# A constant product ahead of each score unit of the second layer, in a two-layer gated attention kernel

## The chip, the cores and the metric

One core of one Trainium2 chip. The metric is the device time in microseconds (us). The engines are named as in the profile: PE is TensorE (PEld its weight loads), DVE is VectorE, ACT is ScalarE, POOL is GpSimd, SP is SyncE.

## The reference

Sixteen sequences of 128 rows and 128 features go through two gated blocks. Each block is a cross-attention to a context of 120 rows (16 heads of 8), added to x with a gate, and then a feed-forward part, added with a gate. The feed-forward of layer 0 is a mixture of 8 experts of which two are taken, that of layer 1 a mix of each row with the one before it. Only layer 0 masks the keys.

```python
x = x + tanh(g_xattn[0]) * L0_xattn(layernorm(x), ctx, ctx, mask, ...)   # q, k, v, softmax over 120 keys, out
x = x + tanh(g_ffn[0])   * L0_moe(layernorm(x), ...)
x = x + tanh(g_xattn[1]) * L1_xattn(layernorm(x), ctx, ...)              # no mask
x = x + tanh(g_ffn[1])   * L1_mix(layernorm(x), ...)                     # sigmoid(r) * (relu(k)**2 @ Wv)
```

## The kernel before, in words

The whole program is written out by hand, one function per engine, with semaphores between them. Each engine runs its instructions in the order in which they are written. A layer's attention is a pipeline over steps, `s` from 0 to B + 5 (B is 16); sequence `s` of the layer enters the pipeline in step `s`. A step has four units, `r` from 0 to 3, of four heads each.

What TensorE does for one sequence is spread over several steps:
- `scores_q` (L974) computes the scores with the queries as rows, four products of 128x120 into bank 0 or 1. It waits with `max_done` until VectorE's row maximum of two units earlier (L454) has read that bank. Layer 0 adds a product for the mask ahead of the four (L986).
- VectorE splits the negated maxima into three bf16 parts (L471 to L493), TensorE transposes them (`turn_max`, L1022), ScalarE copies them (L771), and GpSimd issues three DMAs that put them as three more rows into the tile of the queries (L368).
- `scores_k` (L994) runs 10 units (LAG) behind `scores_q` and computes the scores again with the keys as rows, with the maxima subtracted by those three rows, into bank 2 or 3. It waits for the DMAs (`m_ld`) and for the exponentials of two units earlier (L780). Layer 0 has a product for the mask here too (L1005).
- `values` (L1038), four steps behind, multiplies by the values; `turn_back` (L1046) turns the result; VectorE divides by the sums (L483, L489); `turn_ctx` (L1055) and `out_proj` (L1059) follow, and VectorE adds to x (L500).

A group is four sequences. While a group is in the pipeline, the next one is prepared, by `prep` (L1061), in 16 units numbered u = 4p + r, spread over four steps. `prep_at` (L196) gives the group and the p of a step: in layer 1 step 0 has p = 1, so that steps 3 and 7 begin a new preparation, and steps 11 to 15 have none. Key products stand in units 1, 4 and 5 (bank 6), the turn of the normalised x in unit 3 (L947, bank 7), query products in units 5, 6 and 8 (L955, L959, bank 7), value projections in unit 10 (L966, bank 6). Bank 7, the query bank, is read by ScalarE after unit 3 (L744) and twice after the query products (L751), and a last time by VectorE in unit 9 (`last_q`, L519). `q_reader` holds the last reader's semaphore and count, and `bank_read` (L926) waits for it.

TensorE runs a unit in this order: `scores_q`, then `turn_max`, then `scores_k`, and then the rest.

Of the kernel before, what the change touches and what calls it, by code (L numbers as in the profile page):

```python
# [40 lines left out]
BF16 = mybir.dt.bfloat16  # L41
# [5 lines left out]
B, S, SK, D = 16, 128, 120, 128  # L47
# [8 lines left out]
UNITS, UH = 4, 4  # L56
# [10 lines left out]
def gated_blocks(nc, x, ctxT, mask, wts, w2sh, bcols, brows, gates, ident, identh, negidh, sel, rank, onesrows, out):  # L67
    ctx = ExitStack()
    with ctx:
        def sb(name, shape, dt=F32):  # L70
            return ctx.enter_context(nc.sbuf_tensor(name, shape, dt))

        def sem(name):
            return ctx.enter_context(nc.semaphore(name))
# [18 lines left out]
        epsT = sb("epsT", [128, GB])  # L93
        warm = sb("warm", [128, GB])
        powT = sb("powT", [128, GB])

        st6 = sb("st6", [S, GB, 6])
        mv = sb("mv", [S, GB, 2])
# [69 lines left out]
        q_st = sem("q_st"); q_ld = [[sem(f"q_ld{i}{f}") for f in range(2)] for i in range(2)]  # L168
        k_done = sem("k_done"); k_evac = sem("k_evac")
        k_st = sem("k_st"); k_ld = [[sem(f"k_ld{i}{f}") for f in range(2)] for i in range(2)]  # L170
        v_done = sem("v_done"); v_evac = sem("v_evac"); bo_done = sem("bo_done"); bo_ok = sem("bo_ok")
        qm_done = sem("qm_done"); max_done = sem("max_done"); nm_ok = sem("nm_ok")
        nt_done = sem("nt_done"); nt_evac = sem("nt_evac"); m_ld = [sem("m_ld0"), sem("m_ld1")]
        km_done = sem("km_done"); exp_done = sem("exp_done")
# [228 lines left out]
        def _(v):  # L403
# [112 lines left out]
            def last_q(G):  # L516
                v.wait_ge(q_done, PARTS * (G + 1))
                L = G // NG
                nc.vector.tensor_scalar(qp[:, PARTS - 1, :], QB[:, :], BC[:, 2 * L:2 * L + 1], None, ALU.add).then_inc(q_evac, 1)  # L519

            ln(0, 0)
            ln_apply(0, 0)
            v.wait_ge(w_in, 64)
# [395 lines left out]
        def _(pe):  # L919
# [6 lines left out]
            def bank_read(reader):  # L926
                if reader[0]:
                    pe.wait_ge(*reader[0])

            def k_proj(G, p):  # L930

                L, g = G // NG, G % NG
                if p == 0:
                    bank_read(kv_reader)
                    mm(KVB[:, 0:GK], W(WK[L]), CT[:, g * GK:(g + 1) * GK], start=True, stop=True).then_inc(k_done, 1)  # L935
                    kv_reader[0] = (k_evac, PARTS * (G + 1))
                else:
                    pe.wait_ge(k_evac, PARTS * G + p)
                    mm(KVB[:, 0:GK], NEG[:, :], kp[:, p - 1, :], start=False, stop=True, skip_group_check=True).then_inc(k_done, 1)
# [231 lines left out]
            for L in range(LAYERS):  # L1171
                for u in range(UNITS):
                    prep(L * NG + 1, u)
                for s in range(B + 6):
                    G, p = prep_at(L, s)
                    for r in range(UNITS):
                        if s < B:
                            scores_q(L * B + s, r)
                        if r == (2 if s > 1 else 0) and 1 <= s < B + 1:
                            turn_max(L * B + s - 1)  # L1180
                        U = UNITS * s + r - LAG
                        if 0 <= U < B * UNITS:
                            scores_k(L * B + U // UNITS, U % UNITS)
                        if r == 1 and 6 <= s < B + 3:
                            out_proj(L * B + s - 6)
                        if r == 0 and 4 <= s < B + 4:
                            values(L * B + s - 4)
                        if r == 2 and 4 <= s < B + 4:
                            turn_back(L * B + s - 4)
                        if r == 3 and 5 <= s < B + 4 or r == 0 and s == B + 4:  # L1190
                            turn_ctx(L * B + s - 5 if r == 3 else L * B + B - 1)
                        if r == 1 and s == B + 4:
                            out_proj(L * B + B - 1)
                        if G is not None:
                            prep(G, UNITS * p + r)
                        if r == 3 and ffn_turn_at(s) is not None:
                            turn(2 * L + 1, ffn_turn_at(s))
                        if L == 0 and r == 0 and ffn_turn_at(s - 1) is not None:
                            logits(ffn_turn_at(s - 1))
                        if L == 1 and s == 0:  # L1200

                            moe_out(NG - 1, r)
                    if L == 0 and s == 1:
                        pe.wait_ge(w_in3, 16)
                        bias_product(0)
                        bias_product(1)
                    if L == 0 and s == 8:
                        pe.wait_ge(w_in2, 80)
                    if L == 0 and s == B + 1:
                        pe.wait_ge(max_done, B * UNITS)  # L1210
                        hidden(0, 0)
                        hidden(0, 1)
                    if L == 1 and s == FILL - 1:
                        kr_mix(0)
                    if L == 1 and s == FILL:
                        kr_mix(1)
                    if s in (B + 2, B + 3):
                        out_proj(L * B + s - 5)
                    if L == 1 and s == FILL:
                        v_mix(0)  # L1220
                if L == 0:
                    pe.wait_ge(exp_done, B * UNITS)
                    turn_gates(0)
                    for k in range(2, NBLK + 1):
                        hidden(0, k)
                    for g in range(NG - 1):
                        for k in range(NBLK + 1):
                            if k < NBLK and (g, k) != (2, 0):
                                gate_rows(g, k)
                            hidden(g + 1, k)  # L1230
                            if (g, k) == (2, 0):
                                gate_rows(g, k)
                            if g == 0 and k == 2:
                                turn(1, NG - 1)
                            if g == 2 and k == 1:
                                turn(2, 0)
                            if g == 2 and k >= 2:
                                q_proj(NG, k - 2)
                        if g == 0:
                            logits(NG - 1)  # L1240
                        if g in (0, 2):
                            turn_gates(g + 1)
                        if g < NG - 1:
                            for i in range(GB):
                                moe_out(g, i)
                        if g == 1:
                            turn_gates(g + 1)
                    for k in range(NBLK):
                        gate_rows(NG - 1, k)

                    pe.wait_ge(h_act, NG * (NBLK + 1))
                    kv_reader[0] = (gt_evac, NG)
                else:
                    v_mix(1)
                    kr_mix(2)
                    turn(3, NG - 1)
                    v_mix(2)
                    kr_mix(NG - 1)
                    v_mix(NG - 1)
# [65 lines left out]
```

## Time and profile before

| | us |
|---|---|
| median of 3 runs | 351.34 |
| lowest and highest run | 346.81 and 354.74 |
| the profiled execution | 347.46 |
| its span, first to last instruction | 345.5 |
| TensorE busy | 277.3 (80%) |
| VectorE busy | 211.6 (61%) |
| ScalarE busy | 171.2 (50%) |
| GpSimd busy | 90.4 (26%) |
| mean granted TensorE clock | 0.922 of full |

The span falls into layer 0's attention (to about 155 us), layer 0's experts (to about 212), layer 1's attention (to about 322) and layer 1's mix. A busy TensorE is not one at its peak, since matmuls overlap in the array and their ends are modelled; so what it waits for, the clock that it was granted, and the chain that ends last say more than its share. The granted clock has two levels: 1.00 is 2.4 GHz, 0.50 is 1.2 GHz.

### The profile page before, as it was taken

What the parts mean: (1) busy time and instruction counts of PE and PEld (TensorE: products, weight loads), DVE (VectorE), ACT (ScalarE), POOL (GpSimd) and SP (SyncE); (2) the same over time, 40 slices, a digit from 0 to 9 for tenths busy, and PEclk for the clock granted to TensorE, in tenths of its full rate; (3) what the DMA queues carried; (4) which work ended last, traced back from release to release, by engine and by line L of the source; (5) the groups of instructions that cost most, each with busy time, mean ns of one, the idle gap of its engine ahead of it and who ended that gap; (6) DMA issues with size and microseconds to landing.
All of it is one profiled execution on the core that took longest, in us unless ns stands there. A gap on an engine that the chain in (4) does not pass through costs nothing.

```text
span 345.5 us, 7867 instructions
## 1 busy us (share of the span) xinstructions
PE 277.3 (80%) x2967; PEld 207.1 (60%) x2980; DVE 211.6 (61%) x653; ACT 171.2 (50%) x330; POOL 90.4 (26%) x156
## 2 busy tenths in 40 slices
PE   1624789999999999868999979898888778888681
PEld 0312556777777777655657557567667567766561
DVE  2412776677584685662557457856877866738752
ACT  1410236656665565636742722446676565576220
POOL 3500233322431241111001102414234333342420
PEclk9955989999999999998999999759999998899878
DMA  8475546443343340000000142433545340000022
GB/s 232 111 196 163 136 135 191 136 129 108 107 132 100 98 117 18 4 2 0 2 0 1 45 124 88 137 126 94 144 130 141 118 127 5 2 5 2 0 63 62
DMA packets 27663, 30.48 MB, mean 88 GB/s; under 512 B 13699, under 2 KB 24804, under 8 KB 26468
## 3 DMA queue, kind: packets, MB, share of 16 engines
q1 hardware_dynamic: 20366, 27.11, 27.2%
q10 hardware_dynamic: 4188, 2.47, 2.8%
q0 software_dynamic: 3072, 0.40, 0.8%
q8 instruction: 24, 0.39, 0.5%
q14 instruction: 13, 0.11, 0.1%
HBM read 22.43 MB, written 7.14 MB: 86 GB/s over the span
## 4 chain that ended last, share of the span: by engine, by line
PE 53%; DVE 16%; DMA 13%; issue 8%; ACT 4%; POOL 3%; ACTq 1%; SPq 1%; another core or an unknown queue 0%; DVEq 0%; POOLq 0%
DMA QS<-nmT 8%; PE bank L1038 6%; PE bank L990 5%; PE bank L1009 5%; PE bank L1125 4%; PE bank L986 3%; PE bank L1005 3%; PE bank L1046 3%; PE bank L1077 3%; DMA QS<-qparts 3%; PE bank L955 2%; PE bank L947 2%; DVE st L427 2%; DVE nmx L454 2%; PE bank L1059 2%
## 5 line engine op out<-in xcount | busy, mean ns | idle before, releaser
L454 DVE TENSOR_REDUCE nmx<-bank 128x4 f32<-128x480 f32 x128 | 81.3, 652 | 43.1 <-PE bank L990 42.7
L780 ACT ACTIVATE P<-bank 120x512 f32<-120x512 f32 x128 | 76.4, 598 | 31.9 <-PE bank L1009 30.5
L368 POOL DMA_DIRECT2D QS<-nmT x96 | 47.4, 498 | 139.6 <-ACT nmT L771 139.3
L990 PE MATMUL bank<-KS,QS 72*128 72x120 bf16 x512 | 51.3, 226 | 4.7 <-DVE nmx L454 3.2
L1009 PE MATMUL bank<-QS,KS 75*120 75x128 bf16 x512 | 53.2, 229 | 2.1 <-DMA QS<-nmT 2.0
L990 PEld LDWEIGHTS bank<-KS,QS 72*128 72x128 bf16 x512 | 39.7, 103 | 24.1 <-issue 10.4
L1009 PEld LDWEIGHTS bank<-QS,KS 75*120 75x120 bf16 x512 | 46.2, 140 | 10.3 <-issue 2.8
L1038 PE MATMUL bank<-P,VS 120*32 120x128 f32 x1024 | 36.3, 284 | 6.4 <-DVE cn L489 4.5
L986 PE MATMUL bank<-MB,IDH 128*128 128x480 bf16 x64 | 24.7, 386 | 13.3 <-DMA QS<-qparts 9.8
L1038 PEld LDWEIGHTS bank<-P,VS 120*32 120x32 f32 x1024 | 27.7, 113 | 9.5 <-ACT P L780 6.0
L500 DVE SCALAR_TENSOR_TENSOR X<-bank,TG,X 128x128 f32<-128x128 f32 x32 | 11.0, 345 | 28.3 <-PE bank L1059 28.2
L787 ACT ACTIVATE cx<-bank 128x512 f32<-128x512 f32 x32 | 19.1, 595 | 17.4 <-PE bank L1038 17.4
L758 ACT ACTIVATE kp<-bank,BC 128x480 bf16<-128x480 f32 x16 | 10.6, 660 | 34.1 <-PE bank L935 15.2
L445 DVE TENSOR_SCALAR xn<-X,mv,rstd 128x128 f32<-128x128 f32 x64 | 19.5, 368 | 12.4 <-POOL rstd L338 12.4
L336 POOL TENSOR_TENSOR ve<-mv,epsT 128x4 f32<-128x4 f32 x16 | 3.2, 197 | 90.5 <-DVE mv L431 90.5
L1005 PE MATMUL bank<-IDH,MB 128*120 128x512 bf16 x64 | 25.7, 402 | 1.0 <-DMA QS<-nmT 0.9
L1046 PE MATMUL bank<-IDF,cx 128*128 128x128 f32 x128 | 20.1, 280 | 1.5 <-ACT cx L787 1.4
L771 ACT ACTIVATE nmT<-bank 48x128 bf16<-48x128 bf16 x32 | 8.6, 268 | 20.5 <-PE bank L1022 20.5
L935 PE MATMUL bank<-CT,WT 128*128 128x480 f32 x16 | 10.3, 729 | 9.8 <-DMA NEG<-in_negidh 7.6
L1077 PE MATMUL bank<-XT,WT 128*128 128x512 f32 x32 | 17.1, 627 | 0.9 <-ACT FF L839 0.8
L579 DVE TENSOR_TENSOR FF<-bank,FF 128x512 f32<-128x512 f32 x16 | 10.7, 688 | 10.9 <-remote 6.0
L1125 PE MATMUL bank<-WT,FF 128*128 128x128 f32 x128 | 17.0, 276 | 0.0
(119 smaller groups left out, 442.1 us busy)
## 6 DMA issues: line engine op xcount, KB each, us to landing
KS<-kparts SPq DMA_DIRECT2D x48, 180.0 KB
QS<-qparts SPq DMA_DIRECT2D x42, 192.0 KB
kparts<-kp SPq DMA_DIRECT2D x24, 120.0 KB, 2.8
qparts<-qp SPq DMA_DIRECT2D x21, 128.0 KB, 3.5
QS<-nmT POOLq DMA_DIRECT2D x96, 4.0 KB, 2.4
QS<-qparts ACTq DMA_DIRECT2D x6, 192.0 KB
out<-X SPq DMA_DIRECT2D x4, 256.0 KB, 2.3
X<-in_x SPq DMA_DIRECT2D x3, 256.0 KB, 13.8
```

Of the source, the lines that this page charges most:

```text
L368: po.dma_start(QS[G % 2][STACK + p:STACK + p + 1, k // 2, :, (k % 2) * S:(k % 2 + 1) * S], nmT[Bi % 2][p * H:(p + 1) * H, :]).then_inc(m_l ...
L445: ins = nc.vector.tensor_scalar(xn[:, i, :], X[:, GB * g + i, :], mv[:, i, 0:1], rstd[:, i:i + 1], ALU.subtract, ALU.mult)
L454: ins = nc.vector.tensor_reduce(nmx[Bi % 2][:, UH * r:UH * r + UH], bank[U % 2][:, 0:UH * SK].rearrange("p (h k) -> p h k", k=SK), AX.X, A ...
L780: nc.scalar.activation(P[Bi % 2][:, hh, :], src, ACT.Exp, scale=SCALE).then_inc(exp_done, 1)
L986: mm(o[:, 0:UH * SK].rearrange("p (h k) -> p h k", k=SK), IDH[:, :], MB[:, b, :].unsqueeze(1).broadcast_to([S, UH, SK]), start=True, stop= ...
L990: last = mm(o[:, j * SK:(j + 1) * SK], QS[G % 2][0:STACK, k // 2, h, (k % 2) * S:(k % 2 + 1) * S], KS[G % 2][0:STACK, k // 2, h, (k % 2) * ...
L1005: mm(o[0:SK, :].rearrange("p (h s) -> p h s", s=S), MB[:, b, :], IDH[:, :].unsqueeze(1).broadcast_to([S, UH, S]), start=True, stop=False, ...
L1009: last = mm(o[0:SK, j * S:(j + 1) * S], KS[G % 2][0:ROWS, k // 2, h, (k % 2) * SK:(k % 2 + 1) * SK], QS[G % 2][0:ROWS, k // 2, h, (k % 2) ...
L1038: last = mm(bank[4][VW * j:VW * (j + 1), r * S:(r + 1) * S], VS[G % 3][:, k, h, :], P[Bi % 2][:, h, :], start=True, stop=True, skip_group_ ...
L1046: last = nc.tensor.transpose(bank[4][:, r * S:(r + 1) * S], cx[Bi % 2][:, r * S:(r + 1) * S], IDF[:, :])
L1077: mm(bank[j % 2][:, :], W(W1 + k), XT4[:, g, :], start=True, stop=True).then_inc(h_done, 1)
L1125: last = mm(bank[4][:, i * D:(i + 1) * D], lhs, rhs, start=(k == 0), stop=(k == NBLK))
```

## The change

A tile `idle` of 128x512 bf16 is set to ones once, as the first instruction on VectorE. In layer 1 (`L == 1`), ahead of `scores_q`, TensorE multiplies 128 columns of it with all of it and writes the result to bank 7, where nothing reads it. It does so in each unit of steps 0 to 15, except in units 3 to 9 of a preparation, in which bank 7 is in use. That makes 44 products. Each waits for the memset and for the last reader of bank 7.

```diff
         epsT = sb("epsT", [128, GB])
         warm = sb("warm", [128, GB])
         powT = sb("powT", [128, GB])
+        idle = sb("idle", [128, 512], BF16)

         st6 = sb("st6", [S, GB, 6])
         mv = sb("mv", [S, GB, 2])
...
         q_st = sem("q_st"); q_ld = [[sem(f"q_ld{i}{f}") for f in range(2)] for i in range(2)]
         k_done = sem("k_done"); k_evac = sem("k_evac")
         k_st = sem("k_st"); k_ld = [[sem(f"k_ld{i}{f}") for f in range(2)] for i in range(2)]
-        v_done = sem("v_done"); v_evac = sem("v_evac"); bo_done = sem("bo_done"); bo_ok = sem("bo_ok")
+        v_done = sem("v_done"); v_evac = sem("v_evac"); bo_done = sem("bo_done"); bo_ok = sem("bo_ok"); idle_ok = sem("idle_ok")
         qm_done = sem("qm_done"); max_done = sem("max_done"); nm_ok = sem("nm_ok")
         nt_done = sem("nt_done"); nt_evac = sem("nt_evac"); m_ld = [sem("m_ld0"), sem("m_ld1")]
         km_done = sem("km_done"); exp_done = sem("exp_done")
...
                 L = G // NG
                 nc.vector.tensor_scalar(qp[:, PARTS - 1, :], QB[:, :], BC[:, 2 * L:2 * L + 1], None, ALU.add).then_inc(q_evac, 1)

+            nc.vector.memset(idle[:, :], 1.0).then_inc(idle_ok, 1)
             ln(0, 0)
             ln_apply(0, 0)
             v.wait_ge(w_in, 64)
...
                 if reader[0]:
                     pe.wait_ge(*reader[0])

+            def keep_warm(n):
+
+                pe.wait_ge(idle_ok, 1)
+                bank_read(q_reader)
+                for i in range(n):
+                    mm(QB[:, :], idle[:, 0:128], idle[:, :], start=True, stop=True)
+
             def k_proj(G, p):

                 L, g = G // NG, G % NG
...
                 for s in range(B + 6):
                     G, p = prep_at(L, s)
                     for r in range(UNITS):
+                        if L == 1 and s < B and (G is None or not TURN_STEP <= UNITS * p + r <= Q_STEPS[-1] + 1):
+                            keep_warm(1)
                         if s < B:
                             scores_q(L * B + s, r)
                         if r == (2 if s > 1 else 0) and 1 <= s < B + 1:
```

The next rows are TensorE's order at the start of step 1 of layer 1, from its first score unit on, before the change; L1022 is `turn_max`, L959 the last query product, L966 the value projections.

```order
L990 MATMUL bank0<-KS0,QS0 128x120 x4
L1022 MATMUL bank5<-IDH,nmp0 48x128
L959 MATMUL bank7<-qp,NEG 128x512
L990 MATMUL bank1<-KS0,QS0 128x120 x4
L990 MATMUL bank0<-KS0,QS0 128x120 x4
L966 MATMUL bank6<-WT,CT 120x128 x4
L990 MATMUL bank1<-KS0,QS0 128x120 x4
```

And the same place after it, where all lines of TensorE are 9 higher and L937 is the new product.

```order
L999 MATMUL bank0<-KS0,QS0 128x120 x4
L1031 MATMUL bank5<-IDH,nmp0 48x128
L968 MATMUL bank7<-qp,NEG 128x512
L999 MATMUL bank1<-KS0,QS0 128x120 x4
L937 MATMUL bank7<-idle 128x512
L999 MATMUL bank0<-KS0,QS0 128x120 x4
L975 MATMUL bank6<-WT,CT 120x128 x4
L937 MATMUL bank7<-idle 128x512
L999 MATMUL bank1<-KS0,QS0 128x120 x4
```

The third and the fourth unit now begin with a product into bank 7; the last query product, whose result is still to be read there, stands two units ahead of it.

The last place is step 9 of layer 1, from the end of its second unit to its fourth, after the change.

```order
L1068 MATMUL bank5<-WT,cT1 128x128
L937 MATMUL bank7<-idle 128x512
L999 MATMUL bank0<-KS0,QS0 128x120 x4
L1031 MATMUL bank5<-IDH,nmp0 48x128
L1018 MATMUL bank2<-QS1,KS1 120x128 x4
L1055 MATMUL bank4<-IDF,cx1 128x128 x4
L975 MATMUL bank6<-WT,CT 120x128 x4
L937 MATMUL bank7<-idle 128x512
L999 MATMUL bank1<-KS0,QS0 128x120 x4
```

Before the change the same rows stood there without L937. The product is now ahead of the score products, and of the turn of the maxima, the second score products, the turn back and the value projections behind them.

## Rows read from the trace of the kernel before

**Rows 1.** The page, the chain that ended last, shares by engine

```profile
PE 53%; DVE 16%; DMA 13%; issue 8%; ACT 4%; POOL 3%; ACTq 1%; SPq 1%; another core or an unknown queue 0%; DVEq 0%; POOLq 0%
```

**Rows 2.** Busy time by stretch (columns: stretch, length, busy of each engine, PEclk, DMA share, GB/s)

```profile
core 0: us, PE busy (x) PEld busy (x) DVE busy (x) ACT busy (x) POOL busy (x), PEclk, DMA share, GB/s
...
216.20:219.60 3.40, 1.86 (x24) 1.33 (x25) 2.88 (x8) 0.53 (x3) 0.92 (x2) 1.00 0.67 190
219.60:233.30 13.70, 13.40 (x100) 9.20 (x98) 8.54 (x28) 7.19 (x14) 3.92 (x8) 0.50 0.36 115
233.30:284.50 51.20, 40.77 (x637) 33.90 (x639) 38.11 (x120) 33.13 (x70) 18.18 (x33) 1.00 0.45 127
284.50:287.90 3.40, 3.40 (x45) 2.95 (x46) 1.04 (x4) 1.27 (x3) 0.00 (x0) 0.50 0.06 14
...
294.70:298.10 3.40, 3.32 (x22) 3.17 (x23) 2.77 (x8) 1.47 (x3) 2.53 (x4) 0.50 0.02 4
...
325.40:332.30 6.90, 6.04 (x22) 5.00 (x23) 4.25 (x8) 1.19 (x2) 3.44 (x3) 0.51 0.26 74
```

**Rows 3.** The chain in order of time (start us, us, what), before the first `scores_k`

```profile
215.03 3.85 DMA QS<-nmT
```

**Rows 4.** The chain by line, of 219.6:233.3, 284.5:287.9 and 294.7:298.1 alone

```profile
by line: PE bank L1038 13.6%; PE bank L955 12.6%; issue 12.0%; PE bank L947 7.9%; DVE xn L445 7.8%; POOL rstd L338 7.6%; PE bank L990 7.5%; PE bank L939 7.5%; DVE st L427 6.4%; PE bank L1009 6.2%; DVE nmx L454 5.2%; DVE mv L431 2.8%; POOL v
...
by line: PE bank L1038 56.9%; PE bank L1059 16.1%; PE bank L990 15.1%; PE bank L1009 12.6%; issue 0.7%
...
by line: PE bank L1009 30.5%; PE bank L1046 25.1%; PE bank L947 18.8%; PE bank L990 11.8%; PE bank L1022 7.9%; PE bank L1055 6.3%; issue 4.0%
```

**Rows 5.** The chain in order of time, two of layer 1's value products

```profile
227.76 1.87 PE bank L1038 x32
...
254.02 1.08 PE bank L1038 x32
```

**Rows 6.** Timeline, VectorE: last part of a sequence's maxima (start us, us, instruction)

```profile
62.68 0.17 DVE L493 TENSOR_TENSOR nmp<-nmr,nmp 128x16 bf16<-128x16 f32 x1
...
116.48 0.17 DVE L493 TENSOR_TENSOR nmp<-nmr,nmp 128x16 bf16<-128x16 f32 x1
...
136.88 0.18 DVE L493 TENSOR_TENSOR nmp<-nmr,nmp 128x16 bf16<-128x16 f32 x1
...
220.99 0.18 DVE L493 TENSOR_TENSOR nmp<-nmr,nmp 128x16 bf16<-128x16 f32 x1
...
236.62 0.18 DVE L493 TENSOR_TENSOR nmp<-nmr,nmp 128x16 bf16<-128x16 f32 x1
...
247.82 0.18 DVE L493 TENSOR_TENSOR nmp<-nmr,nmp 128x16 bf16<-128x16 f32 x1
...
260.74 0.18 DVE L493 TENSOR_TENSOR nmp<-nmr,nmp 128x16 bf16<-128x16 f32 x1
...
284.86 0.17 DVE L493 TENSOR_TENSOR nmp<-nmr,nmp 128x16 bf16<-128x16 f32 x1
...
304.10 0.18 DVE L493 TENSOR_TENSOR nmp<-nmr,nmp 128x16 bf16<-128x16 f32 x1
```

**Rows 7.** Timeline, TensorE in layer 0: a mask product and what follows it

```profile
100.18 0.38 PE L1005 MATMUL bank<-IDH,MB 128*120 128x512 bf16 x1
100.40 0.39 PE L1009 MATMUL bank<-QS,KS 75*120 75x128 bf16 x4
```

**Rows 8.** Timeline, steps 5 and 9 of layer 1, around VectorE's last read of bank 7

```profile
237.68 0.75 DVE L519 TENSOR_SCALAR qp<-bank,BC 128x512 bf16<-128x512 f32 x1 [0.31 <-PE bank L959]
...
239.17 0.41 PE L1009 MATMUL bank<-QS,KS 75*120 75x128 bf16 x4 [0.72 <-DMA QS<-nmT]
...
262.30 0.38 PE L990 MATMUL bank<-KS,QS 72*128 72x120 bf16 x4
...
262.77 0.74 DVE L519 TENSOR_SCALAR qp<-bank,BC 128x512 bf16<-128x512 f32 x1
...
263.00 0.22 PE L1022 MATMUL bank<-IDH,nmp 128*48 128x128 bf16 x1 [0.32 <-DVE X L500]
```

**Rows 9.** Timeline, VectorE's first instructions

```profile
4.42 0.87 DVE L427 BATCH_NORM_STATS2 st<-X 128x6 f32<-128x128 f32 x4 [4.42 <-DMA X<-in_x]
```

## The prediction

> **What bounds the kernel now.** I read the page first. TensorE has 53% of the chain of waits, VectorE 16%, transfers 13% [rows 1]. An average says little, so the second view is the table by stretch, cut where the granted clock changes [rows 2]. Layer 2's attention runs from about 213 to 322 us. The reader is to see that it has three stretches at the clock's lower level (0.50, so 1.2 GHz): 219.6 to 233.3, 284.5 to 287.9 and 294.7 to 298.1, 20.5 us in all. In each of them TensorE is busy nearly all the time (13.40 of 13.70, 3.40 of 3.40, 3.32 of 3.40). Just ahead of the first it was busy much less, 1.86 of 3.40. Between the first and the second it kept the full clock for 51 us, busy 40.77 of 51.20, so it idles a fifth of the time there. A fourth low stretch, 325.4 to 332.3, lies behind the last attention step, where VectorE's last layernorm leaves TensorE without work.
>
> The idling has two forms. Ahead of 219 TensorE waits for the first row maxima to arrive by DMA: 3.85 us of the chain from 215.03 [rows 3]. Later it is a ring: score product, row maximum on VectorE, reciprocal, normalised context, value product; TensorE waits briefly at several places of a step of about 6 us.
>
> **Term 1, the clock.** The products lie in steps 1 to 3, 5 to 7 and 9 to 15 of layer 2: 6 ahead of 219.6, 3 in step 3, 9 in steps 5 to 7, 6 in steps 9 and 10, 20 in steps 11 to 15, 44 in all. So they stand in front of all three falls of the clock. Ahead of 219.6 they add about 1 us of work to 1.86, ahead of the other two some two products each. With them the rows ahead of the falls look like the long one that kept its clock, and I expect all three falls to go. What that gives is read from the chain in these stretches alone [rows 4]. In the first, TensorE's lines hold 13.6 + 12.6 + 7.9 + 7.5 + 7.5 + 6.2 = 55% of 13.7 us, 7.6 us; the rest is VectorE, GpSimd and waits. In the second it holds all 3.4 us, in the third nearly all, 3.3. That is 14.3 us of TensorE on the path at the low level. A piece doesn't halve, since part of it is latency: the 32 value products took 1.87 us at the low level and 1.08 at full clock, 42% less [rows 5]; others, of longer streams, come nearer to a half. 14.3 x 0.43 = 6.1 us. Lower bound: the two steps whose maxima's parts are ready at 220.99 and 236.62 took 15.63 us, their like four steps on (247.82 to 260.74) 12.92 [rows 6], so 2.7 us if only these shrink, because the DMA of the row maxima sets the others. Upper bound: all of TensorE's work there (20.1 us) on the path and halved, 10.1.
>
> The Trainium skill, "TensorE: Matmul & The Clock Gate", section "Terms", prices throttled time as that time times the share of pulses left out, which would be 20.5 times a half, 10.2 us. The chain disagrees: 45% of it in the first stretch is VectorE, GpSimd and waits, which the clock does not touch [rows 4]. By the page the kernel would come to 342.7; I go by the chain, and hold the other as a rival.
>
> **Term 2, the products.** None with this operand is in the trace. Its nearest row is the mask product L1005, 128x512 in bf16 with a 128-wide operand: L1005 starts at 100.18 and what follows it at 100.40, 0.22 us on [rows 7]. So 44 x 0.22 = 9.7 us of TensorE's time. How much of it lies on the path? Layer 1 is the experiment: the same step with one mask product ahead of each group of score products, eight per step, none in layer 2. Eight full-clock steps of layer 1 take 53.80 us (62.68 to 116.48), eight of layer 2 24.12 + 24.12 = 48.24 (236.62, 260.74, 284.86) [rows 6]. 64 mask products are 64 x 0.22 = 14.1 us, and cost 5.6: 40%. Late steps hide less: steps 12 to 15 take 20.40 in layer 1 (116.48 to 136.88) and 19.24 in layer 2 (284.86 to 304.10), of which (3.4 + 3.3) x 0.43 = 2.9 is the low clock; 16.3 against 20.4, 4.1 us for 24 mask products of 5.3, 77%. The new product stands ahead of the wait for the row maximum, the mask product behind it, so I take the low end: the 6 ahead of 219.6 hidden under the DMA wait; 18 in steps 3 to 10 at 0.35, 1.4 us; 20 in steps 11 to 15 at 0.7, 3.1 us. Sum 4.5 us. Bounds 0 and 9.7.
>
> **Term 3, the wait for the query bank.** The product writes bank 7, and so waits for its last reader. In unit 10 of each preparation (steps 1, 5, 9, third unit) that is L519, VectorE's evacuation, 0.74 us long. In step 9 the score product L990 started at 262.30, while L519 ran from 262.77 to 263.51 [rows 8]. The new product can start at about 263.56 and L990 at 263.78, 1.5 us later than before. Behind it in TensorE's queue stand turn_max (L1022, 263.00), L1009, the turn back L1046 and four value projections L966, which run without a gap; GpSimd's DMA of the row maxima waits for turn_max, VectorE's next reciprocal for L1046. L1022 had waited 0.32 us for another reason and would now start 1.0 us later, of which 0.2 is the product. In step 5 the same happens (L519 from 237.68 to 238.43), but L1009 waited for a DMA until 239.17 anyway [rows 8]. In step 1 it falls ahead of the 3.85 us that the chain spends on a DMA [rows 3]. So 0.8 for step 9 and 0.2 for step 5: 1.0 us. Bounds 0 and 2.4 (0.8 three times).
>
> **Edits at nothing.** The memset of the 128x512 tile stands first on VectorE, which idles until 4.42 us for its first load [rows 9]. If the cover went, a 512-wide instruction would be late, some 0.7 us by L519. No DMA is added or moved. The wait for the memset is met long before layer 2.
>
> **Sum.** The profiled execution took 347.46 us, 345.5 of it the span. 347.46 - 6.1 + 4.5 + 1.0 = 346.9, 1.3% under the median of the three runs, 351.34. That profile is one of the fastest executions (346.81 to 354.74), and it already has 20.5 us of low clock in layer 2; I read the spread as more or less of such stretches. If so, the change takes the spread away with them and the distance to the median is real, though most of it does not come from this sum.
>
> **Rivals.** A measurement of this kernel can tell about 2%, 7 us, from no change.
> *The low clock is worth half its time.* For: TensorE was busy 20.1 of 20.5 us. Against: TensorE has only 55% of the chain in the first stretch [rows 4]. Gain 10.1, products and waits as above: 342.9; with the products hidden as in the early steps of layer 1 throughout (3.0) 341.4.
> *The clock falls all the same, and the products are paid.* The place is the stretch ahead of 219.6: the first product waits for L519 until 215, and TensorE then stands at the DMA until 219 with the next products done. If these do not hold the clock, those of step 3 and others behind run at the lower level, at twice 0.22, which adds 1 us: 347.46 + 4.5 + 1.0 + 1 = 354.0, and 359.2 with all 44 on the path. It is slower than before from the point where the falls that stay are worth more than 0.6 us, since the two sides of the sum nearly cancel. Against: TensorE at 80% busy kept its clock for 51 us.
> *A fall moves instead of going.* The last low stretch (325.4 to 332.3) follows VectorE's last layernorm, and no product stands there. If the stretches of layer 2 go but another appears at 16 steps or more, 3 of the 6.1 come back: about 350.
>
> **Numbers.** Forecast 0.55, low clock worth half 0.2, clock falls all the same 0.13, a fall moves 0.12. Range 341.5 to 352.5: it takes the first and the last rival in and leaves out the price of all products on the path. Faster by over 2% (under 344.3): the first rival and a little of the forecast, 0.25. Slower by over 2% (over 358.4, or the clock lost and a fast median before): 0.08. Within 2%: 0.67.
>
> **What would show it.** Term 1: the granted clock stays 1.00 from 213 to 322 us, L1038 takes 1.08 throughout, and the parts of steps 2 and 4 (L493) stand about 13 us apart. Term 2: 44 rows of the new product, 0.22 from one start to the next; four steps (5 to 8) take 25 to 26 us, the last steps 4.8 to 5.5 each plus 0.6. Term 3: an idle time of TensorE ahead of the third unit's product in steps 1, 5 and 9 that ends with L519, about 1 us in step 9. The prediction is wrong if a low stretch remains between 213 and 300, or if four steps in the middle take over 27 us.

## The result and the profile after

As in the prediction, layer 1 and layer 2 are from here on the first and the second layer (`L == 0` and `L == 1`), and step n ends when VectorE has the last part of the maxima of sequence n ready. c1 to f4 are the labels of the experiments further down; the changed kernel ran again as d1 and f1.

| | before | changed |
|---|---|---|
| median of the first runs | 349.07 us (4 runs, 345.89 to 354.74) | 351.79 us (4 runs, 351.15 to 352.35) |
| ratio, changed to before | | 1.0151, 95% interval 1.0106 to 1.0195 |
| profiled execution, span, clock | 347.46, 345.5 us, 0.922 | 351.38, 349.4 us, 0.937 |
| all runs of the study, mean | 349.3 us (123 runs, clock 0.919, deviation 3.5) | 349.9 us (22 runs, clock 0.943, deviation 2.0) |

The forecast was 346.9 us and no measurable difference; the first runs came out at 351.8, 1.5% slower. One thing is needed to read this and every ratio below: the comparison leaves out runs over 1.5% above the fastest of their kernel, and since the kernel before scatters from 342 to 359 us and the changed one much less, that takes the upper half from the one and nearly nothing from the other. So each ratio is given with the mean over all runs beside it. By those the change costs 0.5 us, with a 95% interval of -0.5 to 1.6: no difference that 22 runs can show.

The clock of the second layer did most of what was forecast. The table by stretch of the changed kernel, cut as [rows 2] (columns: stretch, length, busy of PE, PEld, DVE, ACT, POOL, then PEclk, DMA share, GB/s):

```profile
216.00:230.10 14.10, 9.52 (x94) 6.76 (x97) 11.70 (x35) 5.48 (x11) 7.01 (x12) 1.00 0.45 125
230.10:233.50 3.40, 3.40 (x45) 2.55 (x45) 1.65 (x6) 1.20 (x3) 0.00 (x0) 0.50 0.50 166
233.50:267.70 34.20, 28.84 (x405) 22.67 (x410) 24.66 (x72) 22.84 (x46) 9.83 (x18) 1.00 0.43 117
267.70:271.10 3.40, 3.40 (x21) 3.06 (x20) 0.24 (x2) 1.19 (x2) 2.72 (x4) 0.50 0.63 192
271.10:326.00 54.90, 46.95 (x691) 38.06 (x697) 39.23 (x128) 34.71 (x71) 18.25 (x31) 1.00 0.14 40
```

Where layer 2's attention had 20.5 us at the lower level, it has 6.8; but low stretches do remain between 213 and 300 us, which the prediction had named as a sign of being wrong. The other profiles agree: in the five with three products or none (before, c1, d2, d3, e4) the attention of layer 2 holds 17.0 to 23.9 us of low clock, in the four with 44 or 88 (the first profile, d1, f1, d4) 3.4 to 6.8. The steps tell what that brought. The last part of a sequence's maxima, as in [rows 6], of steps 0, 4, 8, 12 and 15:

```profile
215.88 0.17 DVE L494 TENSOR_TENSOR nmp<-nmr,nmp 128x16 bf16<-128x16 f32 x1
...
238.78 0.17 DVE L494 TENSOR_TENSOR nmp<-nmr,nmp 128x16 bf16<-128x16 f32 x1
...
263.64 0.17 DVE L494 TENSOR_TENSOR nmp<-nmr,nmp 128x16 bf16<-128x16 f32 x1
...
290.15 0.17 DVE L494 TENSOR_TENSOR nmp<-nmr,nmp 128x16 bf16<-128x16 f32 x1
...
308.52 0.18 DVE L494 TENSOR_TENSOR nmp<-nmr,nmp 128x16 bf16<-128x16 f32 x1
```

And step 0 of before, whose other rows are in [rows 6]:

```profile
212.92 0.17 DVE L493 TENSOR_TENSOR nmp<-nmr,nmp 128x16 bf16<-128x16 f32 x1
```

Against the rows of before: 22.90 us for steps 1 to 4, where it was 23.70 (from 212.92); 24.86 for 5 to 8, where it was 24.12; 26.51 for 9 to 12, where it was 24.12; 18.37 for 13 to 15, where it was 19.24. That is 92.64 against 91.18 over the layer, 1.5 us more. 3.0 us were lost before layer 2's first maxima (215.88 against 212.92), where no product stands, and 0.5 won behind the last, which makes the 3.9 us between the two spans.

All of the 2.4 us in steps 9 to 12 are lost at one place, step 9, which takes 9.05 us where it took 6.29. TensorE in step 9 of the changed kernel, with VectorE's last read of bank 7:

```profile
265.68 0.74 DVE L520 TENSOR_SCALAR qp<-bank,BC 128x512 bf16<-128x512 f32 x1
266.34 0.65 DVE L455 TENSOR_REDUCE nmx<-bank 128x4 f32<-128x480 f32 x1
266.57 0.38 PE L937 MATMUL bank<-idle 128*128 128x512 bf16 x1 [1.20 <-DVE qp L520]
266.79 0.37 PE L999 MATMUL bank<-KS,QS 72*128 72x120 bf16 x4
267.09 0.24 PE L1031 MATMUL bank<-IDH,nmp 128*48 128x128 bf16 x1
...
268.24 1.92 PE L975 MATMUL bank<-WT,CT 128*120 128x128 f32 x8
```

TensorE waits 1.20 us for L520, its next instructions are late as term 3 says, and this time the clock falls a microsecond later, at 267.7: the value projections take 1.92 us where they took 1.04. The product also starts 0.22 us ahead of what follows it, as the mask product did [rows 7].

Where TensorE waits from 215 to 280 us in the changed kernel (waiting line, released by: us, times, longest):

```profile
PE bank L1047 <- DVE cn L490: 2.4, 6, 0.7
PE bank L937 <- DVE qp L520: 2.4, 2, 1.2
PE bank L1018 <- DMA QS<-nmT: 1.4, 1, 1.4
...
PE bank L999 <- DVE qp L520: 0.7, 1, 0.7
```

There are three waits for L520, in steps 1, 5 and 9 (in one the record of the product is missing, and the wait stands at L999), 3.1 us together. None of them stood in the profile before.

### The profile page after: what moved, and what is told of

Read it like the earlier page. It is cut to its first block, busy times and chain, and to the rows that moved or that the text cites. A ratio compares the mean times of both kernels' runs of the same rounds, so it can differ in the third digit from the quotient of the medians.

```text
span 349.4 us, 7990 instructions
## 1 busy us (share of the span) xinstructions
PE 279.9 (80%) x3001; PEld 208.5 (60%) x3024; DVE 212.1 (61%) x654; ACT 172.4 (49%) x330; POOL 90.2 (26%) x156
## 4 chain that ended last, share of the span: by engine, by line
PE 59%; DVE 17%; issue 7%; DMA 7%; ACT 4%; POOL 2%; ACTq 1%; SPq 1%; another core or an unknown queue 0%; DVEq 0%; POOLq 0%
PE bank L999 7%; PE bank L1018 6%; PE bank L1047 6%; DVE nmx L455 4%; PE bank L995 4%; PE bank L1014 4%; PE bank L1055 4%; PE bank L1134 4%; PE bank L1086 3%; DMA QS<-qparts 3%; PE bank L964 2%; PE bank L1068 2%; PE bank L975 2%; DMA QS<-nmT 2%; PE bank L956 2%
## 5 line engine op out<-in xcount | busy, mean ns | idle before, releaser
L999 PEld LDWEIGHTS bank<-KS,QS 72*128 72x128 bf16 x512 | 39.7, 100 | 22.8 <-issue 7.1
L999 PE MATMUL bank<-KS,QS 72*128 72x120 bf16 x512 | 49.7, 221 | 4.3 <-DVE nmx L455 2.1
L1018 PE MATMUL bank<-QS,KS 75*120 75x128 bf16 x512 | 51.3, 223 | 1.4 <-DMA QS<-nmT 1.4
L1018 PEld LDWEIGHTS bank<-QS,KS 75*120 75x120 bf16 x512 | 44.4, 135 | 9.3 <-issue 2.2
L1047 PE MATMUL bank<-P,VS 120*32 120x128 f32 x1024 | 35.6, 281 | 5.7 <-DVE cn L490 3.5
L944 PE MATMUL bank<-CT,WT 128*128 128x480 f32 x16 | 9.2, 661 | 9.7 <-DMA NEG<-in_negidh 7.5
```

The source lines that it names most:

```text
L999: last = mm(o[:, j * SK:(j + 1) * SK], QS[G % 2][0:STACK, k // 2, h, (k % 2) * S:(k % 2 + 1) * S], KS[G % 2][0:STACK, k // 2, h, (k % 2) * ...
L1018: last = mm(o[0:SK, j * S:(j + 1) * S], KS[G % 2][0:ROWS, k // 2, h, (k % 2) * SK:(k % 2 + 1) * SK], QS[G % 2][0:ROWS, k // 2, h, (k % 2) ...
L1047: last = mm(bank[4][VW * j:VW * (j + 1), r * S:(r + 1) * S], VS[G % 3][:, k, h, :], P[Bi % 2][:, h, :], start=True, stop=True, skip_group_ ...
```

## The experiments

Sixteen experiments, fourteen other kernels and twice the changed one, each run 6 or 12 times. They were made in four rounds on four chips; the kernel before ran 29 to 35 times in each, with means of 348.9, 349.1, 349.7 and 349.7 us. The condition for a product is quoted as the change has it; `Q + 1` stands for `Q_STEPS[-1] + 1`. The difference is that of the mean of all runs to 349.3 us, the mean of those 123 runs of the kernel before, with a 95% interval worked out from the two deviations. Taken against the round's own mean a difference moves by at most 0.4 us. c1, which differs from before by a memset alone, is at -1.3, so a single difference of that size shows nothing.

| kernel | products | mean us | clock | difference | ratio (95%) |
|---|---|---|---|---|---|
| c1 memset only | 0 | 348.0 | 0.916 | -1.3 ± 1.6 | 1.0017 (0.9977 to 1.0057) |
| d1, changed | 44 | 349.0 | 0.949 | -0.3 ± 1.1 | 1.0055 (1.0013 to 1.0098) |
| f1, changed | 44 | 350.3 | 0.936 | 0.9 ± 2.0 | 1.0104 (1.0006 to 1.0202) |
| d4 two each | 88 | 350.9 | 0.948 | 1.6 ± 1.3 | 1.0111 (1.0069 to 1.0152) |
| e2 half length | 41 | 349.4 | 0.933 | 0.1 ± 1.5 | 1.0126 (1.0018 to 1.0235) |
| c2 none in unit 10 | 41 | 349.2 | 0.934 | -0.2 ± 1.8 | 0.9995 (0.9946 to 1.0043) |
| d2 unit 10 alone | 3 | 350.4 | 0.920 | 1.0 ± 1.9 | 1.0002 (0.9950 to 1.0055) |
| d3 its wait alone | 0 | 350.2 | 0.917 | 0.8 ± 1.9 | 1.0002 (0.9937 to 1.0068) |
| f2 steps 5 to 10 | 13 | 348.0 | 0.929 | -1.4 ± 2.1 | 0.9994 (0.9931 to 1.0056) |
| c3 steps 11 to 15 | 20 | 347.3 | 0.931 | -2.0 ± 1.1 | 0.9996 (0.9957 to 1.0035) |
| c4 steps 1 to 3 | 9 | 347.5 | 0.938 | -1.9 ± 1.4 | 1.0000 (0.9957 to 1.0042) |
| e3, ends only | 28 | 346.2 | 0.939 | -3.1 ± 1.1 | 1.0028 (0.9964 to 1.0091) |
| f4, ends again | 28 | 347.4 | 0.939 | -2.0 ± 1.2 | 0.9981 (0.9928 to 1.0034) |
| e1 even units | 20 | 346.5 | 0.932 | -2.9 ± 1.3 | 1.0021 (0.9963 to 1.0079) |
| f3 ends, even | 14 | 346.9 | 0.932 | -2.5 ± 1.6 | 0.9981 (0.9932 to 1.0031) |
| e4 tail fill | 12 others | 348.7 | 0.919 | -0.6 ± 1.6 | 1.0057 (0.9996 to 1.0118) |

**Are the 3 us ahead of layer 2 the memset?** c1 keeps the tile and the memset and drops all products.

```diff
-                        if L == 1 and s < B and (G is None or not TURN_STEP <= UNITS * p + r <= Q + 1):
+                        if False and L == 1 and s < B and (G is None or ...):
```

> The changed kernel with the tile and its memset, but none of the 44 products. If the 3 us that the changed kernel's profile loses ahead of layer 2 come from the memset (or from what it moves at the start): 3 us slower than before, ratio 1.008 or more, and the step in which the clock falls in layer 1 is late as there. If they are only where the clock happened to fall in that execution: ratio 1.000 within 0.004.

Measured: ratio 1.0017. No cost of the memset is seen (3 us were expected if it had one), and c1's profile has the maxima of step 0 of layer 2 ready at 213.56 us. The profiles of this study have them ready anywhere from 212.5 to 221.2 us, and this goes with where the clock fell ahead of them. From the last maxima of layer 1 to the first of layer 2 they take 75.8 to 76.9 us with 3.4 us of low clock between (eleven profiles), 77.1 to 77.8 with 6.8, 79.3 and 79.7 with 13.6, and 82.0 with 17.0. The changed kernel's first profile took 101.8 us for the sixteen maxima of layer 1 and before 99.3, and it has two low stretches there where before has one; e1, e2 and f4, with the same two, took 101.3 to 102.5. So a single comparison holds noise of 3 us or more from the part ahead of layer 2.

**Does unit 10 make it slower?** c2 leaves the three products out, d2 keeps only them, d3 keeps only their wait, and d1 and f1 run the changed kernel again.

```diff
-(G is None or not TURN_STEP <= UNITS * p + r <= Q + 1)
+(G is None or not TURN_STEP <= UNITS * p + r <= Q + 2)              # c2
+G is not None and UNITS * p + r == Q + 2                            # d2, d3
-                            keep_warm(1)
+                            bank_read(q_reader)                     # d3
```

> The three products in unit 10 of a preparation left out (steps 1, 5, 9), 41 remain. Theory A, the wait for the query bank (L520 in the changed kernel) costs 1.2 us in step 9 and starves TensorE so that its clock falls at 267.7: step 9 takes 6.3 us instead of 9.05, no low stretch between 234 and 300, the kernel 2.5 to 3 us faster than the changed one, so about 349. Theory B, the length of the products is the price: 3 x 0.22 at most, 351.

> The changed kernel once more, beside the kernel before on this chip. Theory A (the unit-10 products are what made it slower): 351 to 352, ratio 1.010 to 1.018, as at first. Rival (the four runs of the first look fell unluckily): ratio 1.000 to 1.006, like the kernel without those three products.

> Only the three products of unit 10 (steps 1, 5, 9). Theory A: each waits for VectorE's last read of bank 7; step 9 takes 7.3 to 9 us instead of 6.3, and the layer gets 1 to 4 us longer: ratio 1.003 to 1.012. Rival (what counts is the length of all 44): same as before, 3 x 0.22 us at most.

> No product at all; the score product of unit 10 waits for the last read of bank 7 in steps 1, 5 and 9. Theory A: it costs the same as d2 less 0.2 to 0.6 us, since the wait is the price and the product is not. Rival: same as before, and the product itself is the price.

> The changed kernel a third time. Net-zero theory (5 us of clock gained, 5 us of price): mean of all runs within 1 us of the mean of before, clock 0.945 to 0.95. Rival (it is slower, as in the first four runs): 2 us or more above before.

The wait is there, and it needs no product: in d3, which has none, TensorE waits three times for L520, 1.1 us in steps 1 and 9 and 0.4 in step 5.

```profile
PE bank L999 <- DVE qp L520: 2.6, 3, 1.1
```

Step 9 takes 7.21 us in d3 and 7.50 in d2 and d1, against 6.29 before and 6.3 to 6.7 in the ten other profiles without a wait for L520 there, c2 excepted. These are d3's rows for steps 8 and 9, then d1's:

```profile
263.92 0.18 DVE L494 TENSOR_TENSOR nmp<-nmr,nmp 128x16 bf16<-128x16 f32 x1
...
271.13 0.18 DVE L494 TENSOR_TENSOR nmp<-nmr,nmp 128x16 bf16<-128x16 f32 x1
```

```profile
262.98 0.18 DVE L494 TENSOR_TENSOR nmp<-nmr,nmp 128x16 bf16<-128x16 f32 x1
...
270.49 0.18 DVE L494 TENSOR_TENSOR nmp<-nmr,nmp 128x16 bf16<-128x16 f32 x1
```

In the time of the whole kernel it is small: d2 and d3 together, 24 runs, stand 0.9 us above before (± 1.4), c2 0.7 us under the changed kernel. So the cost of theory A is shown in step 9, about 1 us, and not in the time of the whole kernel, whose interval takes in nothing. The 2.5 to 3 us that I expected of it in c2 did not come, for two reasons. The low stretch inside step 9 was that one execution's (d1 and f1 took 7.5 us there at full clock), and c2's own step 9 took 7.71 us, because the DMA of the maxima was late: `PE bank L1018 <- DMA QS<-nmT: 1.4, 1, 1.4` in its waits. The changed kernel itself came out at 349.0 in d1 and 350.3 in f1. The first four runs, 351.2 to 352.4, stand 2.3 us above the mean of these 18 (349.4); whether that was chance or the place where they ran is not shown.

**Step 1, where I took the wait as hidden.** The chain in order of time of d1, step 1:

```profile
216.86 0.67 DVE qp L520
217.53 0.14 issue
217.67 0.38 PE bank L937
218.04 0.21 PE bank L999 x4
218.26 1.63 PE bank L975 x8
219.88 0.43 PE bank L937
220.31 0.40 PE bank L999 x4
220.71 0.43 PE bank L937
221.14 0.40 PE bank L999 x4
```

L520 is on the chain, and a DMA of the maxima only from 225.01 on: behind the wait come the value projections and three products with the clock at 0.50 from 218.3 to 221.7. Steps 1 to 3 take 16.38 us in d1 and 16.56 in f1 (14.34 before), and 14.33 in c2 and 14.35 in f4, which have no product in unit 10. But d3, the wait alone, takes 14.55 there, and d2, the product with its wait, 16.20. Of the six profiles with a product in unit 10 of step 1 five have a low stretch that begins in that step, at 215.7 to 218.3, and take 16.0 to 17.0 us; the first profile of the changed kernel has none there and takes 15.27. None of the twelve others has a fall in step 1, and they take 14.2 to 15.4. So what step 1 loses is not the wait alone: it is the product behind it and the clock that falls with it, and the runs don't tell these two apart.

**What does a product cost?** d4 doubles all, e2 halves their length.

```diff
-                            keep_warm(1)
+                            keep_warm(2)                                                      # d4
-                    mm(QB[:, :], idle[:, 0:128], idle[:, :], start=True, stop=True)
+                    mm(QB[:, 0:256], idle[:, 0:128], idle[:, 0:256], start=True, stop=True)   # e2, with c2's condition
```

> Two products in place of each one (88, 9.5 us more of TensorE's time). If the exposed share is what the changed kernel's profile suggests at full clock (four steps in the middle 24.86 us against 24.12 for 13 products, 0.26 of their length): 2.5 to 4 us slower than the changed kernel, clock 0.01 higher. If steps are bound by TensorE: up to 9 us slower.

> 41 products (none in unit 10) of 256 columns in place of 512. If the price is their length: half the price of the run without unit 10, and if the clock needs only some of that work, it stays at 0.93 and the kernel is 1 to 2 us faster than before. If a product costs by its place in the queue and not by its length: as slow as that run, with less clock, so 1 us slower than before.

Steps 13 to 15 are the cleanest place, since there are profiles with the full clock throughout and no, one or two products per unit. In order, the maxima of steps 12 and 15: d2 without, with steps 13 and 14 between, c3 with one, d4 with two.

```profile
287.83 0.17 DVE L494 TENSOR_TENSOR nmp<-nmr,nmp 128x16 bf16<-128x16 f32 x1
...
293.92 0.18 DVE L494 TENSOR_TENSOR nmp<-nmr,nmp 128x16 bf16<-128x16 f32 x1
...
300.55 0.17 DVE L494 TENSOR_TENSOR nmp<-nmr,nmp 128x16 bf16<-128x16 f32 x1
...
305.55 0.18 DVE L494 TENSOR_TENSOR nmp<-nmr,nmp 128x16 bf16<-128x16 f32 x1
```

```profile
287.32 0.17 DVE L494 TENSOR_TENSOR nmp<-nmr,nmp 128x16 bf16<-128x16 f32 x1
...
305.70 0.17 DVE L494 TENSOR_TENSOR nmp<-nmr,nmp 128x16 bf16<-128x16 f32 x1
```

```profile
289.61 0.17 DVE L494 TENSOR_TENSOR nmp<-nmr,nmp 128x16 bf16<-128x16 f32 x1
...
308.75 0.18 DVE L494 TENSOR_TENSOR nmp<-nmr,nmp 128x16 bf16<-128x16 f32 x1
```

17.72 without, 18.38 with 12 products (18.37 to 18.39 in seven profiles), 19.14 with 24. Twelve products are 2.6 us long and cost 0.66, a quarter; the next twelve cost 0.76. In steps 5 to 8, where no profile has low clock, five profiles with eight or nine products take 24.8 to 25.1 us and eight without products or waits 23.5 to 24.5: on the mean 0.9 us for 2.0 us of products. d4's next nine cost 1.1. Doubling gave 1.6 us over before and 1.1 over the changed kernel, less than the 2.5 that I expected at least, and the clock no higher: in d4's profile one low stretch of 3.4 us was left in layer 2's attention, as in d1 and f1. e2 was neither: the same as before within its error, and not faster as hoped; its profile kept a low stretch of 13.7 us in steps 2 to 4.

**What does the low clock cost?** The same rows tell, if a step is compared with itself. Before, from the maxima of step 2 to those of step 4, then of steps 13 and 14 (the rows around them are in [rows 6]):

```profile
227.26 0.17 DVE L493 TENSOR_TENSOR nmp<-nmr,nmp 128x16 bf16<-128x16 f32 x1
...
292.46 0.18 DVE L493 TENSOR_TENSOR nmp<-nmr,nmp 128x16 bf16<-128x16 f32 x1
...
299.10 0.17 DVE L493 TENSOR_TENSOR nmp<-nmr,nmp 128x16 bf16<-128x16 f32 x1
```

And d1, steps 2, 3 and 4, all at full clock:

```profile
225.56 0.17 DVE L494 TENSOR_TENSOR nmp<-nmr,nmp 128x16 bf16<-128x16 f32 x1
...
231.84 0.17 DVE L494 TENSOR_TENSOR nmp<-nmr,nmp 128x16 bf16<-128x16 f32 x1
...
238.07 0.18 DVE L494 TENSOR_TENSOR nmp<-nmr,nmp 128x16 bf16<-128x16 f32 x1
```

The length of a step in us, and in brackets how much of it the clock was at its lower level:

| step | before | d2 | e4 | d1 | d4 |
|---|---|---|---|---|---|
| products per unit here | 0 | 0 | 0 | 1 | 2 |
| 3 | 6.27 (6.3) | 6.28 (6.3) | 6.27 (6.3) | 6.28 (0) | 6.27 (0) |
| 4, none in any | 9.36 (6.0) | 8.23 (3.9) | 8.42 (4.0) | 6.23 (0) | 6.08 (0) |
| 13 | 7.60 (3.0) | 6.09 (0) | 6.09 (0) | 6.32 (0) | 6.59 (0) |
| 14 | 6.64 (3.4) | 6.63 (0) | 6.63 (2.3) | 6.62 (0) | 6.63 (0) |
| 15 | 5.00 (0) | 5.00 (0) | 7.64 (7.6) | 5.44 (0) | 5.92 (0) |

Steps 3 and 14 take the same at either level and with any number of products; over all 18 profiles step 14 takes 6.62 to 6.64, step 3 6.26 to 6.28 (6.57 once). Steps 7, 8 and 10 vary as little. So TensorE's speed does not set their length there; which wait does was not tested. Steps 4 and 13 lose half a microsecond for each one that before has at the lower level: (9.36 - 6.23) / 6.0 = 0.52 and (7.60 - 6.09) / 3.0 = 0.50. (f3, with low clock in step 3 and none in step 4, takes 6.62 in step 4, so some 0.4 us of the first may come from step 3.) The loss is not in proportion, though: c1 has the lower level all through step 13 and takes 7.65 us, hardly more than before with 3.0 us of it, and c4 and e4 lose 2.64 us to 7.6 in step 15. It depends on what stands in the low part. So the 20.5 us of low clock in before's layer 2 cost 3.1 us in step 4 and 1.5 in step 13, 4.6 in all, and the third stretch, which lies in step 14, cost nothing.

**Where is gain and where is price?** c3, c4, e3 and f4 have products at the ends of the layer only, f2 in the middle only, e1 and f3 in the first and third unit of a step only.

```diff
-if L == 1 and s < B and (...)
+if L == 1 and 11 <= s < B and (...)                                        # c3
+if L == 1 and s < 4 and (...)                                              # c4
+if L == 1 and s < B and (s < 4 or s > 10) and (... Q + 2)                  # e3, f4
+if L == 1 and 4 <= s <= 10 and (... Q + 2)                                 # f2
+if L == 1 and s < B and r % 2 == 0 and (... Q + 2)                         # e1
+if L == 1 and s < B and (s < 4 or s > 10) and r % 2 == 0 and (... Q + 2)   # f3
```

> Only the 20 products of steps 11 to 15. Price theory of the prediction: 3 us on the path against 2.9 of clock, the same as before (349). If they are cheaper than I had it (the changed kernel took 18.37 us for steps 12 to 15 against 19.24): 1 to 2 us faster than before.

> Only the 9 products of steps 1 to 3. Clock theory: the 13.7 us stretch at 219.6 shrinks to one of 3.4 or goes, steps 2 to 4 take 13 to 14 us instead of 15.6, and the rest is as before: 1 to 2.5 us faster than before. Rival: nothing is won, since the step is set by the DMA of the row maxima: the same as before.

> Products only in the first and third unit of a step, none in unit 10: 20 products. Slot theory: in these units TensorE waits behind the score product anyway (for the normalised context, for the sum into x), so they cost nothing, while the clock gains half of what all 44 do (granted clock 0.93 to 0.935 against 0.919 before): 1.5 to 2.5 us faster than before. Rival: price and gain go hand in hand wherever the products stand: the same as before.

> Steps 1 to 3 and 11 to 15 without unit 10: 28 products, the two places where before's low stretches lay. If the price lies in the middle and at unit 10, and the gain at the ends: clock 0.94, 2 to 3 us faster than before. Rival: the same as before.

> Only the products of steps 5 to 10, none in unit 10: 13. Middle theory: a price without a gain, since no low stretch lay there: 1 to 2 us slower than before at the same clock (0.92), the four steps 5 to 8 take 24.8 us instead of 24.1. Rival (price spread evenly over all 44): 0.5 us slower at most.

> Steps 1 to 3 and 11 to 15, first and third units only: 14 products. If half of the work holds the clock: clock 0.93 to 0.935, mean 346 to 347, as good as 28 products. If the clock needs them all: like before, 349.

> The 28 products of steps 1 to 3 and 11 to 15 again. Ends theory: mean 346 to 347, 2.5 to 3 us (0.8%) under the mean of before on this chip. Rival (the first was luck of the placement): within 1 us of before.

Each of these versions is below the mean of before, those with the ends or the even units by 2 to 3 us; e3 and f4 together, 24 runs, by 2.6 us (0.7%) with an interval of 1.6 to 3.5. By the ratios none of them differs from the quicker half of before (every interval takes in 1). So they seem to make the kernel steadier and its mean a little lower, but its best runs no faster. Fewer products also reach the clock: f3, with 14, comes to 0.932 and e1, with 20, to 0.932. f4's table by stretch shows 6.8 us of low clock in layer 2's attention:

```profile
216.00:230.60 14.60, 10.81 (x110) 7.96 (x111) 12.34 (x38) 5.58 (x11) 6.83 (x12) 1.00 0.39 112
230.60:237.40 6.80, 6.41 (x56) 4.48 (x57) 3.59 (x9) 2.83 (x5) 0.18 (x1) 0.50 0.45 129
237.40:329.60 92.20, 74.73 (x1096) 60.63 (x1103) 66.70 (x211) 56.93 (x118) 31.90 (x55) 1.00 0.26 73
```

The middle theory fell: f2 was not slower than before. Its steps 5 to 8 do take 25.01 us, as expected, but steps 9 to 15 were short in that execution, and over 12 runs the clock was 0.929 and no loss is seen (-1.4 ± 2.1).

**The low stretch of the tail.** e4 drops all 44 and puts 12 products where TensorE idles behind the last output projection.

```diff
                             out_proj(L * B + B - 1)
+                            if L == 1:
+                                for i in range(12):
+                                    mm(bank[4][:, :], idle[:, 0:128], idle[:, :], start=True, stop=True)
```

> None of the 44; in their place 12 products in a row into bank 4 behind the last output projection, where TensorE idles 3 us while VectorE does the last layernorm, and ahead of a low stretch of 6.8 us that all profiles have. If TensorE's work there is on the path and the stretch goes: 2 us faster than before (6.8 x 0.3), clock 0.935. Rival: the fall comes from time before the gap too, or the products delay the next ones: the same as before or 0.5 us slower.

The low stretch around 325 to 332 us went, but another lay ahead of it:

```profile
298.40:315.50 17.10, 15.91 (x160) 13.67 (x164) 7.01 (x23) 8.09 (x18) 4.43 (x9) 0.50 0.02 4
315.50:346.20 30.70, 23.26 (x217) 17.06 (x210) 21.40 (x53) 12.48 (x24) 8.28 (x9) 1.00 0.12 35
```

From the last maxima (308.35) to the end are 41.05 us, 10.3 of them at the lower level, since the tail begins inside that stretch; before it was 41.4 with 9.9. So this profile does not test what full clock in the tail is worth. The profiles together do: seven with 7 to 8 us of low clock in the tail take 39.5 to 40.4 us for it, nine with 10 take 40.7 to 41.8, c2 with 11.2 takes 41.9 and c4 with 16.4 takes 43.85; a straight line through the 18 rises by 0.46 us for each. The twelve runs of e4 differ neither from before (-0.6 ± 1.6) nor in their clock (0.919); whether the products gave anything there stays open.

## Why the prediction was wrong

From the forecast, 346.9, to the first four runs, 351.8, are 4.9 us. The base of the sum, 347.46, lay 1.9 under the mean of before, the balance of the three terms was off by 1.1, and the four runs stand another 1.9 above the mean of all 22 runs of the changed kernel. The last part says nothing of the mechanism; the first two are the steps that failed.

**The base.** The sum starts from one execution of 347.46 us, and I called the distance to the median, 1.3%, real, because the change would take the spread away. 347.46 lies 1.9 us under the mean of 123 runs. The spread did shrink, from 3.5 to 2.0 us, but from both ends: the changed kernel has no runs of 355 and none under 346.8 either, while before has some of 342 to 345. A product is paid in every execution, and how much it brings depends on where the clock would have fallen; that would explain the missing fast runs, and the ratios above 1 with them, but no run shows it.

**Term 1, the clock.** The mechanism was right, the size was not. The low clock in front of which products stand became shorter: over all runs the clock rose from 0.919 to 0.943, which in a 347 us span is 2 x 0.024 x 347 = 16.7 us less at the lower level. But a microsecond of it is worth less than the 6.1 / 20.5 = 0.30 us of the prediction. Stretch by stretch, the 6.1 were 3.3 (7.6 x 0.43) for the first, 1.5 for the second and 1.4 for the third. Measured are 3.1, 1.5 and nothing, 4.6 in all or 0.22 for each microsecond. So the step that failed in this term is the third stretch: TensorE holds nearly all of the chain there [rows 4], and yet step 14 takes 6.62 to 6.64 us at either level. A chain shows what ended last, not by how much. The 123 runs of before agree with the average: a straight line through their times and clocks falls by 150 us per unit of clock (95% interval 121 to 184), and 0.01 of clock are 6.9 us at the lower level, so 1.5 / 6.9 = 0.22 (0.17 to 0.27). It explains under half of their scatter (correlation -0.68), and it counts low clock anywhere in the kernel, also the 17 us between 18 and 36 us that 16 of the 18 profiles have; c3 and d1 are without it and have the first maxima no earlier than the others. By 0.22 the gain is 3.6 us, not 6.1. The lower bound beside it (2.7) compared steps 3 and 4 with steps 7 and 8 and so saw the first stretch alone. The Trainium skill's price for throttled time ("TensorE: Matmul & The Clock Gate", section "Terms") is 0.5 us each here. Steps 4 and 13 of before agree with it (0.52 and 0.50), the layer does not, since steps 3 and 14 give nothing, and nor does step 13 of c1 (1.6 us for 7.7).

**Term 2, the products.** 4.5 us was the sum. Late steps cost 0.25 of the products' length, not 0.7. The prediction took 16.3 us as the full-clock time of steps 13 to 15, and it is 17.7; so layer 1's mask products there cost 2.7 us of 5.3, half and not 77%, and the new product, ahead of the wait for the maximum, costs half of that again. Middle steps cost 0.45, above the 0.35 taken. At these shares it is 20 x 0.22 x 0.25 + 18 x 0.22 x 0.45 = 2.9 us.

**Term 3, the wait.** That the wait comes, and where, is shown by d3: three waits of 0.4 to 1.1 us that no product is needed for. Step 9 loses 0.9 to 1.2 us, where 0.8 were worked out; in step 5 (6.40 to 6.76 us with the wait, d4 aside, and 5.76 to 6.67 without) nothing can be told. The failing part is step 1, taken as hidden behind the DMA: with the product behind the wait steps 1 to 3 lose up to 2.2 us, most often with the clock low, while the wait alone lost 0.2. Over 24 runs of the wait or its product the kernel's time shows 0.9 ± 1.4.

**The sum.** Gain 3.6, and a difference of +0.5 ± 1.0 over all runs: so the price was about 4.1, where 5.5 were forecast. 2.9 for the products and 1 to 1.5 for the wait agree with that. The balance was forecast at -0.6 and is +0.5 ± 1.0, so its sign is not settled. That gain and price nearly cancel was forecast rightly, with both of them taken too high; that is luck in part.

**The rivals.** The low clock at half its time: no for the layer, about that within steps 4 and 13 of before. The clock falls all the same: no in layer 2 as a whole, though it fell in step 9 of the first profile behind the new wait. Its 354.0 is nearer to the first runs than the forecast, but not for its reason. A fall moves: partly, in d1 and f1 one stretch of 3.4 us now lies in step 1. Its 350 is the mean of the changed kernel by chance, since it was worked out for a fall behind step 16.

## What to carry to other kernels

Filling TensorE to hold its clock trades a sure price against an unsure gain, so put fillers only ahead of the places where the clock falls, and never behind a wait that the next real instruction does not have: in step 9 one such product cost 1.2 us, and the twelve of steps 13 to 15 cost 0.66. Read the worth of the clock from the same step at either level in several profiles, not from the pieces of one chain, and check it against how the kernel's own times follow its granted clock over many executions. And take the base of a sum from the mean of such runs, since one profile can lie 2 us off it.

## What was not expected of the hardware

A filler is cheap: 0.22 us of TensorE's time cost 0.055 us in steps 13 to 15, where TensorE is busy 13.02 of 17.72 us without them (d2). Five of the fifteen steps take the same within 0.03 us whether TensorE's clock is at 1.2 or 2.4 GHz and with no, one or two fillers per unit, as far as the profiles have these cases (one step of one profile excepted), while step 4 lost 3.1 us to 6.0 at the lower level and step 13 1.5 to 3.0. And where the clock falls within layer 1 and the experts differs from one execution to the next, so that step 0 of layer 2 ends anywhere from 212.5 to 221.2 us in kernels that are alike up to there, except for one memset.
